# Weight pieces of 2048 columns, and twelve chunks of the first FFN tile convolved on TensorE

## The reference, cut to what matters

```
x = x + layernorm(attn(layernorm(x)))             # stage A: u, gates, scan h = a*h + b*u, W_out
def weight_quant(w):                              # one scale for a whole weight matrix
    scale = 1.0 / clip(mean(abs(w)), 1e-5)
    return clip(round(w * scale), -1, 1) / scale
h = bit_linear(x, w1)                             # 1024 -> 4096 channels
h = conv1d(h, conv_w, taps=3, padding=1, per channel) + conv_b
h = silu(h)
out = bit_linear(h, w2)                           # 4096 -> 1024
x = x + layernorm(out)
```

## Time and profile before

| | us |
|---|---|
| median of 3 runs (lowest to highest) | 1293.35 (1292.61 to 1295.97) |
| the profiled execution | 1298.81 |
| its span on the slowest core (core 1) | 1297.2 |
| spans of the eight cores | 1288.8 to 1297.2 |
| PE busy | 1145.6 (88%) |
| DVE busy | 1069.1 (82%) |
| ACT busy | 912.2 (70%) |
| POOL busy | 413.1 (32%) |

### The profile page before, as it was taken

How to read it: one execution, slowest core, us unless ns; L and a number is a source line. 1 busy time by engine, 2 the same in 40 slices (tenths; PEclk the granted TensorE clock), 3 DMA queues, 4 the chain that set the end, 5 groups by cost and what they waited for, 6 DMA issues and landing times.

```text
span 1297.2 us, 17964 instructions; the slowest of 8 cores (1288.8 to 1297.2 us)
## 1 busy us (share of the span) xinstructions
PE 1145.6 (88%) x5896; PEld 583.9 (45%) x5896; DVE 1069.1 (82%) x2187; ACT 912.2 (70%) x1217; POOL 413.1 (32%) x647
## 2 busy tenths in 40 slices
PE   0378799988665789999999999999999999999997
PEld 0256667765222334444444444444444444444443
DVE  0268889986998899999989998998999899878761
ACT  0798989998798787677767767777776776666101
POOL 1124222221774113334433334433333442212232
PEclk9987878888899899999999999999999999999899
DMA  9997579994763112221222211121221111000122
GB/s 204 317 327 228 173 243 308 317 312 160 248 188 113 39 25 79 56 61 58 71 77 61 78 58 57 57 90 58 77 62 57 57 58 58 33 34 33 65 66 81
DMA packets 69867, 153.79 MB, mean 119 GB/s; under 512 B 34448, under 2 KB 34448, under 8 KB 69520
## 3 DMA queue, kind: packets, MB, share of 16 engines
q1 hardware_dynamic: 69344, 150.03, 37.2%
q0 software_dynamic: 432, 2.62, 1.2%
HBM read 114.36 MB, written 33.55 MB: 114 GB/s over the span
## 4 chain that ended last, share of the span: by engine, by line
PE 67%; DVE 14%; ACT 8%; DMA 4%; issue 3%; SPq 2%; POOL 1%; DVEq 0%; POOLq 0%; ACTq 0%
PE pF L877 32%; PE pO L728 27%; DMA stg<-w1T 4%; PE pF L328 3%; SPq L73 2%; PE pO L374 2%; DVE h L776 2%; DVE h L781 1%; DVE xs L395 1%; DVE hsc L358 1%; ACT w2q L547 1%; ACT h L788 1%; POOL kw L540 1%; ACT kw L543 1%; ACT hp L734 1%
## 5 line engine op out<-in xcount | busy, mean ns | idle before, releaser
L877 PE MATMUL pF<-w2q,h 128*128 128x512 fp8e4 x1984 | 465.5, 380 | 0.7 <-DVE h L856 0.7
L728 PE MATMUL pO<-xqT,w1q 128*128 128x512 bf16 x1792 | 426.9, 382 | 13.6 <-ACT hp L734 8.6
L877 PEld LDWEIGHTS pF<-w2q,h 128*128 128x128 bf16 x1984 | 194.2, 98 | 233.3 <-issue 4.3
L728 PEld LDWEIGHTS pO<-xqT,w1q 128*128 128x128 fp8e4 x1792 | 175.4, 98 | 229.8 <-issue 23.4
L734 ACT ACTIVATE hp<-pO 128x512 bf16<-128x512 f32 x224 | 133.3, 595 | 158.6 <-PE pO L728 158.6
L776 DVE SCALAR_TENSOR_TENSOR h<-hp,cwt,h 128x512 bf16<-128x512 bf16 x256 | 198.0, 774 | 36.3 <-ACT h L766 35.7
L753 ACT ACTIVATE bt<-hp,cwt 128x512 bf16<-128x512 bf16 x256 | 183.9, 718 | 7.0
L788 ACT ACTIVATE h<-h 128x1024 bf16<-128x1024 bf16 x128 | 134.6, 1051 | 60.1 <-DVE h L781 59.5
L849 DVE TENSOR_TENSOR h<-h,bc 128x512 bf16<-128x512 bf16 x256 | 143.9, 562 | 0.0
L781 DVE TENSOR_TENSOR h<-h,bt 128x512 bf16<-128x512 bf16 x256 | 131.2, 512 | 15.0 <-ACT bt L753 1.7
L908 POOL TENSOR_SCALAR sm<-sm 128x1 f32<-128x1 f32 x32 | 16.7, 521 | 357.4 <-DVE sm L900 357.4
(11 more groups left out here) (149 smaller groups left out, 1527.6 us busy)
## 6 DMA issues: line engine op xcount, KB each, us to landing
stg<-w1T SPq DMA_DIRECT2D x40, 512.0 KB, 10.7
xs<-x SPq DMA_DIRECT2D x32, 512.0 KB, 8.3
stg<-w2T SPq DMA_DIRECT2D x32, 512.0 KB, 7.5
x2c<-xs SPq DMA_DIRECT2D x32, 512.0 KB, 8.5
stgC<-w2T SPq DMA_DIRECT2D x32, 512.0 KB, 5.2
x2r<-x2c SPq DMA_DIRECT2D x31, 512.0 KB
out<-yev SPq DMA_DIRECT2D x30, 512.0 KB, 2.9
x2q<-x2c SPq DMA_DIRECT2D x28, 512.0 KB, 3.7
```

Of the source, the lines that this page charges most:

```text
L728: p_w1[n] = P(lambda e, k=k: e.matmul(bankW1(n), w1q[:, HD * k + 128 * c:HD * k + 128 * (c + 1)], xT[:, :, k, :], start=(k == 0), stop=(k ...
L877: p_w2[m] = P(lambda e, c=c, jj=jj, hid=hid: e.matmul(pb[:, 512 * jj:512 * (jj + 1)], hid, w2q[:, D * c + 512 * jj:D * c + 512 * (jj + 1)] ...
```

## The change

Two things are changed together.

**Pieces of 2048 columns.** The weights are cut into 16 pieces of 2048 columns for each matrix (`DP`, `NP`). Staging buffers double in width and halve in number (`stg` 4, `stgQ` 3, `stgC` 2, later 3), and `kw` is gone: the first pass writes back in place, and a buffer is free again only when the Sign has read it. The pieces are 64 instead of 128. The generator is called half as often: twice in each of the first eight half steps, then once, and a second time where H % 4 == 3; in the FFN loop at even n. The sum of |w| writes its unused output in 8 bits.

**Twelve chunks on TensorE.** For odd chunks 5 to 27 (`on_pe`) no tap is made on ACT or DVE. DVE builds six diagonal matrices of 128x128 from the taps (each tap split into two bf16 parts), in one instruction of 768 columns, and six matmuls of 128x512 sum the three shifted views of `hp` in `pO`. ACT's SiLU then reads that chunk from PSUM with the bias, and its even neighbour from SBUF.

```diff
@@ staging @@
-    kw = [sb("kw%d" % k, D, F32) for k in range(2)]
-    stgC = [sb("stgC%d" % k, D, F32) for k in range(4)]
+    stgC = [sb("stgC%d" % k, DP, F32) for k in range(3)]
...
-    stg = [sb("stg%d" % k, D, F32) for k in range(8)]
+    stg = [sb("stg%d" % k, DP, F32) for k in range(4)]
...
-    stgQ = [sb("stgQ%d" % k, D, F32) for k in range(7)]
+    stgQ = [sb("stgQ%d" % k, DP, F32) for k in range(3)]
@@ rounded @@
-                t = A(lambda e: e.activation(kf[:, :], src[:, :], AF.Identity, bias=rcc, scale=scale),
-                      kw_free[r], buf[3], v_mean[0], v_mean.get(1))
+                t = A(lambda e: e.activation(src[:, :], src[:, :], AF.Identity, bias=rcc, scale=scale),
+                      buf[3], v_mean[0], v_mean.get(1))
             def sign():
-                kw_free[r] = A(lambda e: e.activation(dst, kf[:, :], AF.Sign, bias=nrc,
-                                                      saturate=False), t, *toks)
-                put(kw_free[r])
+                put(A(lambda e: e.activation(dst, src[:, :], AF.Sign, bias=nrc, saturate=False),
+                      t, *toks))
@@ weight_work @@
-                issue(k + 12)
+                while late:
+                    late.pop(0)()
+                issue(k + 6)
...
@@ half_step @@
-            next(work, None)
             if gs is not None:
                 ln3_max(gs, kqA[gs % 2])
...
-            if H < 8:
+            if H < 8 or H % 4 == 3:
                 next(work, None)
...
-            if H < 8 or H % 2:
-                next(work, None)
@@ new, for the chunks on TensorE @@
+        def on_pe(n):
+            return 4 < n < 28 and n % 2 == 1
...
+        def diagonals(n):
+            d = n // 2 % 4
+            v_dg[n] = V(lambda e: e.tensor_tensor(
+                dg[d][:, :].rearrange("p (s t) -> p s t", s=6),
+                identb[:, :].unsqueeze(1).to_broadcast([128, 6, 128]),
+                cwp[:, 6 * n:6 * n + 6].unsqueeze(2).to_broadcast([128, 6, 128]), OP.mult),
+                v_cwp[0], p_cv[n - 8] if n - 8 > 4 else p_o[NG - 1])
...
+        def conv_pe(n):
+            q.wait("t", v_dg[n], a_ev[n], g_re[n // 4], a_si[n - 4] if n - 4 > 4 else v_x2[NG - 1])
+            for j in range(6):
+                p_cv[n] = P(lambda e, j=j: e.matmul(
+                    bank_cv(n), dg[n // 2 % 4][:, 128 * j:128 * j + 128],
+                    hp3[:, n % 8, j // 2:j // 2 + 512], start=(j == 0), stop=(j == 5)), inc=(j == 5))
...
         def silu(n):
+            if on_pe(n):
+                H_ = h43[:, ring(n - 1), :]
+                A(lambda e: e.activation(H_, H_, AF.Silu), v_cv[n - 1])
+                a_si[n] = a_si[n - 1] = A(lambda e: e.activation(
+                    h43[:, ring(n), :], bank_cv(n), AF.Silu, bias=cbt[:, n:n + 1]), p_cv[n])
+                return
@@ FFN loop @@
+            if on_pe(n - 1):
+                conv_pe(n - 1)
+            if 0 <= n - 1 < NW and not on_pe(n - 1):
                 tap1(n - 1)
...
+            if n == 2:
+                split_taps()
+            if on_pe(n + 1):
+                diagonals(n + 1)
...
-            next(work, None)
+            if n % 2 == 0:
+                next(work, None)
```

More of the change, by code:

```diff
@@ L26 @@
 NH4 = 72
+DP = 2048
+NP = 16
 LAG = 6
@@ L145, in build_program @@
     ysb = [sb("ysb%d" % k, 512, BF16) for k in range(2)]
-    kqA = [stgC[3], sb("kqA1", D, F32)]
+    kqA = [stgC[2][:, D:DP], sb("kqA1", D, F32)]
     xqmA = sb("xqmA", D, BF16)
+    junk8 = nc.alloc_sbuf_tensor_at("junk8", [128, DP], F8, offset=place[0])
     junk = sb("junk", D, BF16)
@@ L171, in build_program @@
     held = sb("held", 32 * 128, BF16)
+    cwp = sb("cwp", 192, BF16)
+    yev_at = place[0]
     yev = [sb("yev%d" % k, D, F32) for k in range(2)]
+    dg = [nc.alloc_sbuf_tensor_at("dg%d" % k, [128, 768], BF16, offset=yev_at + 1536 * k)
+          for k in range(4)]
     x2r = sb("x2r", D, F32)
@@ L519, in mean_end @@
             q.wait("t", v_part[k], pT1_free[0])
-            t = P(lambda e: e.matmul(pT1[:, 0:1], ones[:, :], wsum[:, at + 32:at + 33],
+            t = P(lambda e: e.matmul(pT1[:, 0:1], ones[:, :], wsum[:, at + NP:at + NP + 1],
                                      start=True, stop=True))
@@ L581, in weight_work, with put1, put2 @@
                     buf, at = kept[p] if p in KEEP else (staged[k], at)
[L582 to L586, removed]
-                else:
[L588 to L591, removed]
+                    def put1(t, p=p, buf=buf, at=at):
+                        v_w1q[p] = t
+                        if at == "q":
+                            q_read[p] = t
+                        release(buf, at, t)
+                    rounded(w1q[:, DP * p:DP * (p + 1)], buf, wcons[:, 1:2], pass1[0], put1,
+                            q_read.get(13 + p // 4))
+                else:
+                    def put2(t, p=p, buf=staged[k], at=at):
+                        v_w2q[2 * p] = v_w2q[2 * p + 1] = t
+                        release(buf, at, t)
+                    rounded(w2q[:, DP * p:DP * (p + 1)], staged[k], wcons[:, 3:4], pass1[0], put2,
+                            s_last[p // 4])
+                if p == (10, 15)[h // 2] and len(sums) == NP:
                     mean_begin(sums, h // 2)
@@ L724, in w1_mm @@
             xT = xqT[f % 2].ap().rearrange("p (g k t) -> p g k t", g=4, k=8)
+            if n in (32, 33):
+                q.wait("t", a_si[25], a_si[27])
             q.wait("t", a_t2[4 * f + 3], v_x2[NG - 1] if n in (32, 33) else
@@ L1048, in build_program @@
                            *((p_w1[32 * (gq // 4 - 2) + 31],) if gq >= 8 else d_x2[NG - 2:NG]))
-            cv = n - 1 if 0 <= n - 1 < NW else None
+            cv = n - 1 if 0 <= n - 1 < NW and not on_pe(n - 1) else None
             mq = m + 1 if 0 <= m + 1 < NW else None
```

74 lines of the change are left out of this document (41 added, 33 removed).

## The result

| | before | after |
|---|---|---|
| median (lowest to highest), us | 1294.66 (1292.61 to 1297.93), 4 runs | 1281.08 (1279.08 to 1282.81), 4 runs |
| ratio, 95% interval | | 0.9893 (0.9874 to 0.9912) |
| span of the profiled execution | 1297.2 | 1278.5 |
| spans of the eight cores | 1288.8 to 1297.2 | 1274.3 to 1278.5 |

By the ratio the kernel is 13.9 us faster; 11 were forecast. The sum came out, its two parts did not, so the number is right partly by luck. The table holds means over the eight cores of the start of two instructions, us from the start of the span: the residual of stage A for its output groups 0 to 31 (L395 before, L402 after), and the evacuation of a chunk (L734 before, L741 after).

What follows compares the result with a forecast made beforehand. PE's two products bound the kernel from 467 us on; before that, DVE and ACT fill the first tile and every engine nears its limit in stage A. -9.5 - 2.5 + 1 = -11 us, from 1293.35 to 1282.5 us, range 1276 to 1292.5.

Steps and rivals of the forecast that it cites:

- What bounds the kernel, and where the change acts: Whole kernel: PE's two alternating products bound it from 467 us on; gains or losses arise before and carry through one to one.
- First tile, the sum: First tile: eight chunks take 22.3 us in place of 25.47; twelve odd chunks on TensorE give -9.5 us (-14 to 0).
- First tile, DVE: First tile: DVE needs 20.1 to 21.8 us for eight chunks in place of 24.5, diagonals at 0.9 us each.
- First tile, ACT: First tile: ACT's work for eight chunks falls from 23.2 to 20.8 us; ACT expected to be the busiest engine.
- POOL and the port: First tile: POOL's doubled operations block DVE longer but half as often; no change (-1 to +2 us a stretch).
- Stage A: Stage A: less ACT work gives -2.5 us (0 to -4), the beginning costs +1 (0 to +3).
- the saving of a double instruction: Stage A, ACT: joining two instructions saves 0.19 us per first pass and 0.09 per Sign; with sums, about 12 us of work.
- nearly all off the path: Stage A: of ACT's saving of about 12 us, only 2.5 us counts, where ACT is on the chain of waits.
- loads of 8 KB rows, 4 us: Rival, DMA-bound beginning: longer rows shorten it by 5% or 4 us, giving 1278 or less; chance 2%.
- The beginning: Start of stage A: the first load of 1 MB arrives 1.6 us later, mostly caught up; +1 us (0 to +3).
- Lumps on ACT: Rival, stage A: a double Sign and sum together delay bcg and PE; 14 to 18 us lost, 1296 to 1300; chance 12%.
- PE slows down: Rival, first tile: PE's clock drops after pauses; three slow pairs take back 9 us, eight make it 1298; chance 4%.

Runs made afterwards that it cites:

- The pieces alone: The changed kernel with no chunk convolved on TensorE, all taps as before; pieces of 2048 columns and the generator's new places stay: 1287.21 us, ratio 0.9939 to the kernel before.
- POOL in halves: The changed kernel with POOL's first pass of a weight piece in the first tile as two instructions of 1024 columns: 1279.93 us, ratio 0.9892 to the kernel before.
- Three diagonals: The changed kernel with three diagonals and matmuls per TensorE chunk in place of six, leaving out the taps' low part: 1278.07 us, ratio 0.9875 to the kernel before.
- ACT in halves: The changed kernel with ACT's sums, and in stage A its first passes and Signs, as two instructions of 1024 columns: 1286.68 us, ratio 0.9954 to the kernel before.
- the places alone: The kernel before with narrow pieces, two at each place where the changed kernel has one wide piece, none elsewhere: 1302.36 us, ratio 1.0059.
- the last two experiments: The changed kernel with three diagonals and more chunks on TensorE: odd 5 to 45 (1271.40 us, ratio 0.9827), then all from 6 to 45 (1265.54 us, 0.9755).

## Why the prediction was right, and where it was not

**What bounds the kernel, and where the change acts.** Right. From chunk 46 to 255 the time is 730.1 us before and 730.2 after.

**First tile, the sum (-9.5 us).** The mechanism was right, the size 1.6 times too large. Eight chunks take 22.8 us in the mean (62.7 / 22 x 8) against the 22.3 I took, and 25.3 in place of 25.47 before, -7.0 us over 22 chunks. But no stretch is like the mean: the first eight take 20.8, the next eight 24.9. And I left out the way in: up to chunk 6 the tile loses 2.3 us. The pieces alone lose 1.3 of them. In the chain of waits of the profile after, DVE operations there are held for POOL's wide ones (an L815 of 2.06 us at 330.6, where 0.33 is its time alone), but with POOL in halves 1.7 us are still lost there; this cause stays open.

**First tile, DVE (20.1 to 21.8 us).** Right in the mean, 21.6 us for eight chunks, and for neither stretch: 18.8 and then 24.3. In the second the three convolution groups of four chunks take 12.8 us against my 8.05; more than all the waits came back on them. The diagonals take 0.87 us without a wait, 0.95 in the mean, against 0.9, the six matmuls 1.31 against 1.30.

**First tile, ACT (20.8 us) as the fullest engine.** The size was right, 20.9 us for eight chunks in the mean. That it is the fullest holds for chunks 6 to 14 alone (20.5 of 20.8 us, PE 20.4); from 14 to 22 it is DVE. Three diagonals bear this out: 0.45 us in the first, although they take PE down to 18.3 there, and 3.1 in the second. One limit for all 24 chunks was the wrong picture.

**POOL and the port (no change).** Half right. That the length of POOL's operation does not count is shown: with halves the chunks take 62.9 us. That DVE's waits do not grow is not so from chunk 14 to 22, as said above; why they gather there no run shows. The Trainium skill, SBUF — State Buffer, "Who interferes with whom", has the second operation wait out the first; the longest L826, 2.09 us where 0.42 is its time alone, agrees.

**Stage A (-2.5 + 1 = -1.5 us).** This is the step that failed: 10.2 us. Three terms were wrong. First, the saving of a double instruction: I let the second 1024 columns cost the 0.95 us of a plain SiLU; they cost 0.86 (1.907, 2.091 and 1.997 us against 1.05, 1.23 and 1.14 for a single width). Counted from start to start, as in the prediction (about 0.1 us less than these durations), a first pass saves 0.28 us, not 0.19, a Sign 0.19, not 0.09. Over 19 roundings that is 3 to 4 us of ACT's time more than my 12, so it can't explain the 8.7 by itself. Second, and the main one, "nearly all off the path": it is off the path only in the steady part, where 1.8 us were won. Between groups 0 and 2 I saw only a stretch "bound by the same bytes", but ACT was busy 19.4 of 20 us in it as well; ACT in halves puts 2.2 us back by group 2 and 6.3 by the last. Even in the steady part a block got shorter, where I expected no change: in the means of the eight cores from between 14.75 and 15.05 us to between 14.64 and 14.69. Third, the rows: I gave "loads of 8 KB rows, 4 us" 2%, since nothing in the trace showed it; it was there, 3.4 us (by the rows or by the size of the loads). The first trace could not have shown it, as it has one row length only. That is a reason to put such a term in the sum with its bounds, not to price it at nothing.

**The beginning (+1 us).** Not seen: group 0 starts 0.3 us earlier.

**Lumps on ACT.** They did not bite: stage A's blocks got shorter, and with the places alone stage A ends 0.3 us later. After the change, in one half step of one core below, ACT waits 2.3 us for PE before bcg, more than the 0.61 us of the earlier trace rows, although a Sign and a sum of double width stand before selh (timeline of core 5: start, duration, idle before):

```profile
219.58 1.99 ACT L552 ACTIVATE w1q<-stg,consts 128x2048 fp8e4<-128x2048 f32 x1
...
221.47 1.90 ACT L560 ACTIVATE junk<-stg 128x2048 fp8e4<-128x2048 f32 x1
...
223.36 1.00 ACT L328 ACTIVATE selh<-pF 128x1024 bf16<-128x1024 f32 x1
...
224.27 2.09 ACT L548 ACTIVATE stg<-stg,consts,wcons 128x2048 f32<-128x2048 f32 x1
...
228.68 1.02 ACT L347 ACTIVATE bcg<-pF 128x1024 bf16<-128x1024 f32 x1 [2.33 <-PE pF L335]
```

**PE slows down.** The contrary: from 340 to 400 us the cores' granted clocks are 0.96 to 1.00, before 0.94 to 0.96. Nor did the clock set the pace: in the pieces alone it is 0.83 to 0.91 there, and the 22 chunks take 69.5 us, as before. The prices of this rival did not follow from my own numbers either: a pair at 9.4 us in place of the 5.6 forecast costs 3.8, so three pairs 11 us and eight 31, not 9 and 15.

So the forecast of 1282.5 us stood on two errors of opposite sign, 3.7 us too much in the first tile and 8.7 too little in stage A, and the profiled pair shows 2 us more than the times do. Right for the number, that is luck in part; what was right for its reason is that both changes win, where they act, and that nothing changes after chunk 46.

## What to carry to other kernels

An instruction's fixed part is measured by the difference of two widths of the same operation, not by setting a narrow one against another operation. Where two resources are both nearly full over a stretch, relief of the one that you look at less counts too: ACT's width and the loads each gave part of stage A. Mean busy shares over a whole phase hide who limits it: here ACT and DVE took turns every eight chunks, so one cut gave 0.45 us in one stretch and 3.1 in the next. When an engine has idle banks and time only in one phase, moving work there pays until the next engine is full or the next phase's gate is reached; compute both ahead, since being early at a gate is worth nothing.

## What the runs showed of the hardware that was not expected

Loads of 1 MB with rows of 8 KB per partition moved at 339 to 344 GB/s where loads of 512 KB with rows of 4 KB moved at 329 to 332 (60 to 80 us, DMA share 0.99 to 1.01 on all eight cores at once; in the kernel before, 324 to 332). The step is about as large as the difference between chips: in the last two experiments, on the third chip, the wide loads moved at 330 to 340, and no narrow ones ran there.

In the steady part of stage A the granted clock of PE differed from core to core in the same execution. Before, 260 to 280 us, core 1, then core 4:

```profile
260.00:280.00 20.00, 18.16 (x138) 13.83 (x139) 18.30 (x33) 17.65 (x21) 6.12 (x18) 0.81 0.95 317
```

```profile
260.00:280.00 20.00, 17.12 (x155) 13.71 (x153) 18.62 (x34) 18.71 (x23) 6.80 (x20) 1.00 0.98 329
```

Cores 0 and 1 stood at 0.81 in every 20 us from 180 to 280 us, and ended at 1293.2 and 1297.2 us, the others at 1288.8 to 1293.5. After the change no core did in the stretches from 180, 220 and 260 us. The block of 14.96 us from which I argued was such a core's; in the others a block took 14.75 to 15.05 us in the mean. The longest, 15.05, were core 6's at 0.91 to 1.00, so the clock alone doesn't set a block's length. A clock that the profile of one core shows should be looked up on the other cores before a chain is built on it.
